# Cross-attention and top-2 expert layer: the loads of expert weights and of later context groups move from SyncE's queue to ScalarE's

## The chip, the cores and the metric

The kernel runs on one core of one Trainium2 chip. The metric is the device time of one execution in microseconds (us). The time before is 1234.87 us, the median of three executions (1233.65 to 1238.93 us). All numbers are 32-bit floats but for a few small masks.

## The reference

64 sequences of 128 tokens, 256 wide. The inputs are `x`, `ctx_1024` and the weights:

```python
x = x + xattn(layernorm(x), ctx, ctx)      # 16 heads of 16; Q, K, V, softmax(QK/4) V, Wo, biases
x = x + ffn(layernorm(x))                  # 8 experts, top 2 of 8 per token
# ffn: silu(x Wg[e]) * (x Wu[e]) -> Wd[e], weighted by a softmax over the two best router probabilities
```

Wg and Wu of one expert are 256 x 512, Wd is 512 x 256: 512 KB each, 24 such matrices in all.

## The kernel before, in words

The program is written for each engine by hand: one instruction list for each, with semaphores between them. Nothing is scheduled by a planner. There are two stages.

**Stage A** takes attention and routing, one sequence `i` after another, in 16 groups `g` of 4 (`b` = `i % 4`). It is unrolled. One turn of TensorE (`stage_a`, L666) is: the scores of `i` (L593), the output projection of `i-2`, the values of the next sequence (or, at `b` = 3, the second half of the next group's queries), the attention product of `i-1` (L618), a transposition of the row maxima (L599), a piece of the next group's keys or queries, transpositions of the next group's normalised `x`, and the scores once more, transposed and less their maxima (L607). A turn takes some 7.6 us.

Scores are computed for heads that lie spread over the partitions. SyncE (SP below) does this spreading by DMA: `spread_keys` and `spread_queries` (L302 to L315, issued at L309) copy `kT` and `qT` of sequence `i+1` into the buffer `heads`, two DMAs each, while TensorE works on `i`. For the first sequence of a group, `qT` is complete only after the second query piece was computed at `b` = 3 and copied by ScalarE (`copy_piece`, L906).

SP's list in stage A (L345 to L364) also has, in this order within a group: at `b` = 1 the store of the finished rows (`out<-x`) and the load of `xT`; at `b` = 2 the load of `x` for group `g+2` (`load_x`, L283), which waits for ScalarE's and GpSimd's last reads of `x_sb`; at `b` = 3, between the keys and the queries, the load of the context of group `g+2` (`load_ctx`, L286), which waits until TensorE has computed the last values of the group (`s_v`); and, at every even `i` from 2 to 48, one of the 24 expert matrices (`load_weight`, L297). All DMAs of one engine go through that engine's own queue: SP's is q1 in the profile, ScalarE's q10, GpSimd's q0. The engines' instructions are fetched on q8 and q14.

ScalarE's list (`stage_a`, L932) has, per sequence: two pieces of a normalisation (L865), the copy of V into `v_aug` (`copy_values`, L912, which waits for the product, `s_v`, and for an attention product), two more pieces of a normalisation, squares (L884), the copy of a key or query piece (L906), of transposed rows (L889), and three exponentials (L918). ScalarE issues only four loads in the kernel before, all at the start (L977, L982).

VectorE takes row maxima (L1084), subtracts them (L1091), turns and divides the attention rows, adds the residual, and at `b` = 3 takes statistics of the `x` that `load_x` brought (`first_stats`, L1056). GpSimd writes the routed rows to memory with indirect DMAs.

TensorE's wait that matters for the pieces is at the head of a turn, ahead of the scores:

```python
                    if i > 0:
                        wait(pe, s_vc, i + 1)
                        wait(pe, s_piece_c, min(4 + i, SEQS))
```

**Stage B**, from about 510 us on, runs the experts over the sorted rows, in units of 256 rows. It needs all 24 matrices (`s_experts`); they are there some 110 us earlier.

Of the kernel before, what the change touches and what calls it, by code (L numbers as in the profile page):

```python
# [15 lines left out]
P = 128  # L16
SEQS, TOK, D = 64, 128, 256
HEADS, DK = 16, 16
EXPERTS, F = 8, 512
GROUP = 4  # L20
GROUPS = SEQS // GROUP
DC = D // P
FC = F // P
# [47 lines left out]
def moe_attention(nc, x, ctxT, wq, bq, wk, bk, wv, bv, wo, bo, router, gating, up, down, xT, woT, out):  # L71
# [4 lines left out]
    with ExitStack() as ctx:  # L76
        def sb(name, shape, dt=fp32):
            return ctx.enter_context(nc.sbuf_tensor(name, shape, dt))

        def sem(name):  # L80
            return ctx.enter_context(nc.semaphore(name))
# [10 lines left out]
        gate_sb = sb("gate_sb", [P, EXPERTS * DC * F])  # L92
        up_sb = sb("up_sb", [P, EXPERTS * DC * F])
        down_sb = sb("down_sb", [P, EXPERTS * FC * D])
# [12 lines left out]
        ctxT_sb = sb("ctxT_sb", [P, 2, DC, GROUP * TOK])  # L107
# [93 lines left out]
        def other_bank(i, k):  # L201
            return banks[:, (0 if i % 2 == 0 else 4) + k]

        s_wk, s_wq, s_wv, s_bias, s_bv, s_bo, s_wo, s_wr, s_experts = (sem(n) for n in (
            "wk_loaded", "wq_loaded", "wv_loaded", "bias_loaded", "bv_loaded", "bo_loaded", "wo_loaded", "router_loaded",
            "experts_loaded"))
        s_bv_rep, s_bvo, s_bias_out = (sem(n) for n in ("bv_repeated", "bv_through_wo", "bias_out_ready"))
        s_x, s_xbo = sem("x_loaded"), sem("x_bo_ready")
        s_ctx = [sem("ctx_loaded_0"), sem("ctx_loaded_1")]
# [10 lines left out]
        s_v, s_vc = sem("values_product"), sem("values_ready")  # L220
# [35 lines left out]
        def wait(eng, semaphore, value):  # L256

            if not isinstance(value, int) or value > 0:
                eng.wait_ge(semaphore, value)
# [21 lines left out]
        def _(sp):  # L281
# [3 lines left out]
            def load_ctx(g, u):  # L285
                sp.dma_start(ctxT_sb[:, u], ctxT[:, bass.ds(g * GROUP * TOK, GROUP * TOK)].rearrange(  # L286
                    "(c p) t -> p c t", p=P)).then_inc(s_ctx[u], 16)

            def load_xT(g):
                wait(sp, s_logitT, g)  # L290
                sp.dma_start(xT_sb[:], xT[:, bass.ds(g * GROUP * TOK, GROUP * TOK)].rearrange("(c p) t -> p c t", p=P)).then_inc(s_xT, 16)

            def load_weight(n):
                e, k = divmod(n, 3)
                w_sb, w, c = ((gate_sb, gating, DC), (up_sb, up, DC), (down_sb, down, FC))[k]
                size = w_sb.shape[1] // EXPERTS
                sp.dma_start(w_sb[:, e * size:(e + 1) * size].rearrange("p (c f) -> p c f", c=c),  # L297
                             w[e:e + 1].rearrange("o (c p) f -> p (o c) f", p=P)).then_inc(s_experts, 16)

            def spread(i, o, src, signal):  # L300

                u, b = i // GROUP % 2, i % GROUP  # L302
# [8 lines left out]
            def spread_keys(i):  # L311
                spread(i, 0, kT, s_kh)

            def spread_queries(i):
                spread(i, 1, qT, s_qh)  # L315
# [29 lines left out]
            def stage_a(g, u, far):  # L345
                for b in range(GROUP):
                    i = g * GROUP + b
                    if 0 < i < SEQS - 1:
                        spread_keys(i + 1)
                    if b == 3 and far:  # L350
                        wait(sp, s_v, g * GROUP + GROUP)
                        load_ctx(g + 2, u)
                    if 0 < i < SEQS - 1:
                        spread_queries(i + 1)
                    if b == 1 and g > 0:
                        store_x1(g - 1)
                    if b == 1 and g + 1 < GROUPS:
                        load_xT(g + 1)
                    if b == 2 and far:
                        wait(sp, s_norm, g + 2)  # L360
                        wait(sp, s_xbo, g + 2)
                        load_x(g + 2)
                    if i % 2 == 0 and 2 <= i < 2 + 2 * 3 * EXPERTS:
                        load_weight(i // 2 - 1)  # L364

            for g in range(GROUPS):
                stage_a(g, g % 2, g + 2 < GROUPS)
# [490 lines left out]
        def _(act):  # L858
# [50 lines left out]
            def copy_values(i, bank):  # L909
                wait(act, s_v, i + 1)  # L910
                wait(act, s_att, i - 2)
                nc.scalar.activation(v_aug[:, i % 3, :, 0:DK], bank[:, 0:D].rearrange("p (h r) -> p h r", r=DK),  # L912
                                     ACT.Copy).then_inc(s_vc, 1)
# [12 lines left out]
            def hold(t, u):  # L926
# [2 lines left out]
                nc.scalar.activation(held[u][:, 0:HALF], gate_sb[:, bass.ds(e * HALF, HALF)], ACT.Copy).then_inc(s_held, 1)  # L929
                nc.scalar.activation(held[u][:, HALF:2 * HALF], up_sb[:, bass.ds(e * HALF, HALF)], ACT.Copy).then_inc(s_held, 1)  # L930

            def stage_a(g, u, core, prev, prev2, prev3, nxt, far):  # L932
                for b in range(GROUP):
                    i = g * GROUP + b
                    one, two = (core if b > 0 else prev), (core if b > 1 else prev)
                    if b == 1 and prev2:
                        router_exp(g - 2)
                    if b == 3 and prev2:
                        gap_exp(g - 2)
                    if b == 0 and nxt and g > 0:  # L940
                        first_norm(g + 1, (0, 1))
                    if nxt and b == 3:
                        copy_piece(g + 1, 1 - u, 3, other_bank(i, 1))
                    if b == 2 and prev:
                        second_norm(g - 1, (0, 1))
                    if b < 3:
                        copy_values(i + 1, other_bank(i, 1))
                    if b == 0 and nxt and g > 0:
                        first_norm(g + 1, (2, 3))
                    if b == 3 and core:  # L950
                        square_x1(i - 3)
                    if i == SEQS - 1:
                        act.wait_ge(s_experts, EXPERTS * 3 * 16)
                        act.wait_ge(s_table, EARLY_STEPS)
                        act.wait_ge(s_kh[1], SEQS // 2 * 32)
                        hold(0, 0)
                    if two and b != 2:
                        square_x1(i - 2)
                    if b == 2 and prev:
                        second_norm(g - 1, (2, 3))  # L960
                    if nxt and b < 3:
                        copy_piece(g + 1, 1 - u, b, other_bank(i, 1))
                    if nxt and b == 3:
                        copy_values(i + 1, other_bank(i, 1))
                    if i == 1:
                        copy_normed(1, 0, other_bank(i, 0))
                        copy_normed(1, 1, other_bank(i, 3))
                    if b < 2 and nxt and g > 0:
                        copy_normed(g + 1, b, other_bank(i, 3))
                    if b == 0 and core:  # L970
                        copy_logitsT(g, other_bank(i, 2))
                    softmax_exp(i)
                    if i == 0:
                        first_norm(1, (0, 1, 2, 3))
# [570 lines left out]
```

## Time and profile before

| | us |
|---|---|
| median of three executions | 1234.87 (1233.65 to 1238.93) |
| the profiled execution, its own time | 1237.15 |
| its span, first to last instruction | 1235.4 |
| TensorE (PE) busy | 1200.5, 97% |
| VectorE busy | 652.1, 53% |
| ScalarE busy | 543.9, 44% |
| GpSimd busy | 425.7, 34% |
| mean granted TensorE clock | 0.994 |

"PE" is the matmul part of TensorE, "PEld" its weight load, which overlaps. "SPq" and "ACTq" are the queues of DMA-issuing instructions of SP and ScalarE; such an instruction's time is the time that the engine's instruction stream is held by it, not the time of the transfer. In a list of instructions, a time in square brackets is idle time ahead of the instruction, with what ended it.

### The profile page before, as it was taken

Reading aid. Unit: us, or ns where it says so; the run is one execution under the profiler, and the core shown is the slowest. Engines: PE = TensorE matmul, PEld = TensorE weight load, DVE = VectorE, ACT = ScalarE, POOL = GpSimd, SP = SyncE. Lnnn points to the kernel's source line nnn. Section 1 sums busy time; section 2 is a strip of 40 time slices with the busy share of each in tenths; the row PEclk is TensorE's granted clock in tenths of the full one; section 3 lists DMA queues with packets and bytes.
Section 4 is the critical chain, followed back from the end, with each engine's and each line's share of the span. In section 5 each row is a group of like instructions: output and inputs, shape, how many; then the busy total and the mean of one; then the engine's idle time right before and its main releaser. Section 6 shows DMA issues by size and latency. Waiting matters only on the chain.

```text
span 1235.4 us, 30330 instructions
## 1 busy us (share of the span) xinstructions
PE 1200.5 (97%) x10994; PEld 980.6 (79%) x10995; DVE 652.1 (53%) x1814; ACT 543.9 (44%) x894; POOL 425.7 (34%) x356
## 2 busy tenths in 40 slices
PE   8999999999999999899999999999999999999996
PEld 6677667676767666688888888888888888888995
DVE  3678888888888888734552222222222222222332
ACT  4566666666666665535422222222222222222442
POOL 3211434433434333253554422222232222222332
PEclk9999999999999999899999999999999999999999
DMA  5554556565555443434444433333333333333432
GB/s 157 153 140 140 174 172 174 173 174 169 175 173 174 136 140 102 96 88 65 78 78 79 68 50 51 51 51 51 51 51 51 51 51 51 51 52 39 57 49 31
DMA packets 176432, 121.07 MB, mean 98 GB/s; under 512 B 103840, under 2 KB 159392, under 8 KB 176320
## 3 DMA queue, kind: packets, MB, share of 16 engines
q1 hardware_dynamic: 148832, 81.41, 27.2%
q0 software_dynamic: 26400, 37.09, 17.2%
q8 instruction: 74, 1.21, 0.4%
q10 hardware_dynamic: 1088, 1.05, 0.3%
q14 instruction: 38, 0.31, 0.1%
HBM read 57.24 MB, written 45.46 MB: 83 GB/s over the span
## 4 chain that ended last, share of the span: by engine, by line
PE 91%; DVE 3%; DMA 2%; issue 1%; SPq 1%; ACT 0%; POOL 0%; POOLq 0%; DVEq 0%
PE banks L564 74%; PE banks L593 5%; PE banks L607 5%; PE banks L618 4%; DMA heads<-qT 2%; PE banks L599 1%; DVE row_max L1084 1%; PE banks L570 1%; SPq L309 1%; DMA out<-x_sb,token 1%; PE banks L647 1%; PE banks L747 0%; ACT qT L906 0%; DMA ends<-sorted_x 0%; DVE q_less L1091 0%
## 5 line engine op out<-in xcount | busy, mean ns | idle before, releaser
L513 POOL DMA_INDIRECT out<-x_sb,token x135 | 210.6, 1560 | 418.3 <-DVE x_sb L1434 376.5
L924 ACT ACTIVATE qT<-banks 128x1024 f32<-128x1024 f32 (+1 forms) x75 | 70.4, 939 | 468.9 <-PE banks L564 447.6
L1428 DVE TENSOR_TENSOR heads<-qT,banks 128x1024 f32<-128x1024 f32 (+1 forms) x75 | 83.6, 1115 | 343.5 <-PE banks L564 335.6
L564 PE MATMUL banks<-down_sb,heads 128*128 x1080 | 245.5, 379 | 0.9 <-DVE heads L1428 0.9
L564 PE MATMUL banks<-xnT,kT 128*128 128x256 f32 (+1 forms) x1216 | 244.1, 359 | 0.0
L564 PE MATMUL banks<-xnT,probs 128*128 128x256 f32 (+1 forms) x1184 | 238.4, 359 | 0.0
L564 PEld LDWEIGHTS banks<-xnT,kT 128*128 128x128 f32 x1216 | 213.1, 191 | 25.9 <-issue 0.2
L564 PEld LDWEIGHTS banks<-xnT,probs 128*128 128x128 f32 x1184 | 208.4, 190 | 25.1
L564 PEld LDWEIGHTS banks<-down_sb,heads 128*128 128x128 f32 x1080 | 204.0, 190 | 28.2 <-issue 1.1
L462 POOL DMA_INDIRECT sorted_x<-xn,slots_now x128 | 125.6, 981 | 258.5 <-PE banks L618 82.9
L1084 DVE TENSOR_REDUCE row_max<-banks 128x16 f32<-128x2048 f32 x64 | 146.6, 2290 | 32.5 <-PE banks L593 32.0
L918 ACT ACTIVATE probs<-banks 128x512 f32<-128x512 f32 (+1 forms) x192 | 128.1, 740 | 46.8 <-PE banks L607 46.8
L1434 DVE TENSOR_SCALAR x_sb<-banks,weight 128x256 f32<-128x256 f32 x135 | 59.8, 480 | 123.6 <-PE banks L564 106.3
L593 PE MATMUL banks<-heads 32*128 32x128 f32 x2048 | 74.6, 282 | 9.3 <-DMA heads<-qT 5.4
L607 PEld LDWEIGHTS banks<-q_less,heads 32*128 32x128 f32 x2048 | 64.1, 189 | 19.4 <-issue 16.9
L607 PE MATMUL banks<-q_less,heads 32*128 32x128 f32 x2048 | 76.5, 286 | 1.0 <-DVE q_less L1091 1.0
L593 PEld LDWEIGHTS banks<-heads 32*128 32x128 f32 x2048 | 65.4, 188 | 14.8 <-issue 14.2
L564 PE MATMUL banks<-wo_sb,attnT 128*128 128x265 f32 x256 | 74.6, 414 | 0.0
L618 PEld LDWEIGHTS banks<-probs,v_aug 128*32 128x32 f32 x2048 | 52.0, 109 | 27.7 <-issue 27.0
L618 PE MATMUL banks<-probs,v_aug 128*32 128x128 f32 x2048 | 69.2, 276 | 0.0
L564 PE MATMUL banks<-wv_sb,ctxT_sb 128*128 128x256 f32 x256 | 65.9, 380 | 0.4 <-ACT probs L918 0.4
L1091 DVE TENSOR_TENSOR q_less<-heads,banks 128x256 f32<-128x256 f32 x128 | 48.1, 418 | 33.6 <-PE banks L599 17.2
(187 smaller groups left out, 1237.5 us busy)
## 6 DMA issues: line engine op xcount, KB each, us to landing
xn<-sorted_x SPq DMA_DIRECT2D x240, 64.0 KB
x_sb<-in_x SPq DMA_DIRECT2D x16, 512.0 KB, 4.0
ctxT_sb<-in_ctx SPq DMA_DIRECT2D x16, 512.0 KB
heads<-kT SPq DMA_DIRECT2D x128, 64.0 KB
heads<-qT SPq DMA_DIRECT2D x128, 64.0 KB
xT_sb<-in_xT SPq DMA_DIRECT2D x16, 512.0 KB, 5.5
out<-x SPq DMA_DIRECT2D x16, 512.0 KB
gate_sb<-_L_ffn_kernel_gating_EDF SPq DMA_DIRECT2D x8, 512.0 KB
```

The source lines that it names most:

```text
L462: pool.indirect_dma_start(out=sorted_x[:, :], out_offset=bass.IndirectOffsetOnAxis(ap=slots_now[:, g % 2, i:i + 1], axis=0), in_=xn2[:, g ...
L513: pool.indirect_dma_start(out=out[:, :], out_offset=bass.IndirectOffsetOnAxis(ap=token[:, v, h:h + 1], axis=0), in_=ys[:, 2 * u + h, :], i ...
L564: last = nc.tensor.matmul(dst, lhsT, rhs, start=(i == 0), stop=(i == len(pairs) - 1))
L593: last = nc.tensor.matmul(score_banks(i)[:, j, c * TOK:(c + 1) * TOK], q_heads[strip(j), i % 2, c, :], k_heads[strip(j), i % 2, c, :], sta ...
L607: last = nc.tensor.matmul(score_banks(i)[:, j, c * TOK:(c + 1) * TOK], k_heads[strip(j), i % 2, c, :], q_less[strip(j), c, :], start=True, ...
L618: last = nc.tensor.matmul(bank[32 * j:32 * j + 32, q * TOK:(q + 1) * TOK], v_aug[:, i % 3, 4 * q + j, :], probs[:, j, c, :], start=True, s ...
L918: nc.scalar.activation(probs[:, j:j + n].rearrange("p j h t -> p j (h t)"), score_banks(i)[:, j:j + n], ACT.Exp, scale=DK ** -0.5).then_in ...
L924: nc.scalar.activation(gatedT[:, 0:w * F], all_banks[:, 1024 * place:1024 * place + w * F], ACT.Silu).then_inc(s_silu, 1)
L1084: nc.vector.reduce_max(row_max[:].rearrange("p (j r a) -> p j r a", r=16, a=2)[:, :, 0:4, 1], score_banks(i).rearrange("p j (h t) -> p j h ...
L1091: nc.vector.tensor_tensor(q_less[:, c:c + 2, :], q_heads[:, i % 2, c:c + 2, :], bank[:, 0:TOK].unsqueeze(1).broadcast_to([P, 2, TOK]), ALU ...
L1428: nc.vector.tensor_tensor(fusedT[:, u, 0:w * F], gatedT[:, 0:w * F], gate_up[:, 1024:1024 + w * F], ALU.mult).then_inc(s_fuse, 1)
L1434: last = nc.vector.tensor_scalar(ys[:, 2 * u + h, :], work[:, 0, h * D:(h + 1) * D], weight[:, v, h:h + 1], None, ALU.mult)
```

## The change

`load_weight` and `load_ctx` are issued by ScalarE in stage A, right behind `copy_values`. SP no longer issues the 24 expert matrices nor the contexts of groups 2 to 15; it keeps those of groups 0 and 1. The wait on `s_v` ahead of SP's `load_ctx` goes; `copy_values` has just waited for the same semaphore and value. The context load moves from `b` = 3 to `b` = 2.

```diff
-            def load_weight(n):
...
-                sp.dma_start(w_sb[:, e * size:(e + 1) * size].rearrange("p (c f) -> p c f", c=c),
-                             w[e:e + 1].rearrange("o (c p) f -> p (o c) f", p=P)).then_inc(s_experts, 16)
...
-                    if b == 3 and far:
-                        wait(sp, s_v, g * GROUP + GROUP)
-                        load_ctx(g + 2, u)
...
-                    if i % 2 == 0 and 2 <= i < 2 + 2 * 3 * EXPERTS:
-                        load_weight(i // 2 - 1)
...
+            def load_weight(n):
...
+                act.dma_start(w_sb[:, e * size:(e + 1) * size].rearrange("p (c f) -> p c f", c=c),
+                              w[e:e + 1].rearrange("o (c p) f -> p (o c) f", p=P)).then_inc(s_experts, 16)
+
+            def load_ctx(g, u):
+                act.dma_start(ctxT_sb[:, u], ctxT[:, bass.ds(g * GROUP * TOK, GROUP * TOK)].rearrange(
+                    "(c p) t -> p c t", p=P)).then_inc(s_ctx[u], 16)
...
                     if b < 3:
                         copy_values(i + 1, other_bank(i, 1))
+                    if b == 2 and far:
+                        load_ctx(g + 2, u)
+                    if i % 2 == 0 and 2 <= i < 2 + 2 * 3 * EXPERTS:
+                        load_weight(i // 2 - 1)
```

In SP's list before, at `b` = 2 and `b` = 3 of group 1, to the queries of the next group's first sequence (`heads` is the spread buffer):

```order
L309 DMA heads<-kT 64x256 x2
L309 DMA heads<-qT 64x256 x2
L283 DMA x_sb<-in_x 128x4x256
L297 DMA down_sb<-in_L_ffn_kernel_down_EFD 128x4x256
L309 DMA heads<-kT 64x256 x2
L286 DMA ctxT_sb<-in_ctx 128x2x512
L309 DMA heads<-qT 64x256 x2
```

The same place in SP's list of the changed kernel (its L302 is L309 of before):

```order
L302 DMA heads<-kT 64x256 x2
L302 DMA heads<-qT 64x256 x2
L283 DMA x_sb<-in_x 128x4x256
L302 DMA heads<-kT 64x256 x2
L302 DMA heads<-qT 64x256 x2
```

Between the `x` load and the group's last queries, a weight load and a context load have left SP's list.

ScalarE's list of the changed kernel at `b` = 2 of group 1, from the normalisation to the query copy (its L853, L900, L894 are L865, L912, L906 of before):

```order
L853 ACTIVATE xn<-x,shift,rstd 128x2x4x32 x2
L900 ACTIVATE v_aug<-banks 128x16x16
L928 DMA ctxT_sb<-in_ctx 128x2x512
L924 DMA down_sb<-in_L_ffn_kernel_down_EFD 128x4x256
L853 ACTIVATE xn<-x,shift,rstd 128x2x4x32 x2
L894 ACTIVATE qT<-banks,bq_sb 128x4x128
```

The two DMA rows are new there; the two normalisation pieces and the query copy are behind them. The rest of the list and TensorE's list keep their order.

## Rows read from the trace of the kernel before

**Rows 1.** The page, busy time of the engines.
```profile
PE 1200.5 (97%) x10994; PEld 980.6 (79%) x10995; DVE 652.1 (53%) x1814; ACT 543.9 (44%) x894; POOL 425.7 (34%) x356
```
**Rows 2.** Waits of PE, 0 to 560 us: total, times, longest.
```profile
PE banks L593 <- DMA heads<-qT: 5.4, 7, 1.6
```
**Rows 3.** Busy time by stretch: groups 4 and 5, from scores to scores.
```profile
143.80:175.03 31.23, 30.33 (x466) 21.48 (x467) 27.02 (x80) 20.42 (x43) 12.91 (x12) 1.00 0.59 171
175.03:205.57 30.54, 30.32 (x467) 21.48 (x467) 25.73 (x77) 19.07 (x41) 11.71 (x11) 1.00 0.59 174
```
**Rows 4.** PE in order of time: scores that open a group.
```profile
52.36 1.17 PE L593 MATMUL banks<-heads 32*128 32x128 f32 x32 [0.83 <-DMA heads<-qT]
...
143.82 1.17 PE L593 MATMUL banks<-heads 32*128 32x128 f32 x32 [0.18 <-issue]
175.03 1.17 PE L593 MATMUL banks<-heads 32*128 32x128 f32 x32 [0.85 <-DMA heads<-qT]
...
298.68 1.17 PE L593 MATMUL banks<-heads 32*128 32x128 f32 x32 [1.57 <-DMA heads<-qT]
...
360.15 1.17 PE L593 MATMUL banks<-heads 32*128 32x128 f32 x32 [0.42 <-DMA heads<-qT]
...
422.36 1.17 PE L593 MATMUL banks<-heads 32*128 32x128 f32 x32 [1.21 <-DMA heads<-qT]
```
**Rows 5.** The chain of waits ahead of two such scores.
```profile
80.48 2.02 DMA heads<-qT
...
294.85 3.69 DMA heads<-qT
```
**Rows 6.** SP's queue, group 1 at b=3, then group 4 at b=2 and b=3.
```profile
76.62 1.42 SPq L286 DMA_DIRECT2D ctxT_sb<-in_ctx  x1
79.96 1.11 SPq L309 DMA_DIRECT2D heads<-qT  x2
...
164.05 0.37 SPq L283 DMA_DIRECT2D x_sb<-in_x  x1
...
168.12 0.59 SPq L286 DMA_DIRECT2D ctxT_sb<-in_ctx  x1
171.43 1.10 SPq L309 DMA_DIRECT2D heads<-qT  x2
```
**Rows 7.** DMA queues, 172.2 to 172.6 us: packets, MB, share of 16 engines.
```profile
q8 instruction: 1, 0.02, 16.9%
```
**Rows 8.** DMA queues, 76.4 to 76.8 us.
```profile
q8 instruction: 1, 0.02, 17.5%
```
**Rows 9.** DMA queues, 162.5 to 163.1 us.
```profile
q8 instruction: 1, 0.02, 15.2%
```
**Rows 10.** DMA queues, 285.6 to 286.0 us.
```profile
q8 instruction: 1, 0.02, 21.0%
```
**Rows 11.** ScalarE in order of time, group 4, b=2.
```profile
162.75 0.39 ACT L912 ACTIVATE v_aug<-banks 128x256 f32<-128x256 f32 x1
163.03 1.09 ACT L865 ACTIVATE xn<-x,shift,rstd 128x256 f32<-128x256 f32 x2
165.79 0.69 ACT L906 ACTIVATE qT<-banks,bq_sb 128x512 f32<-128x512 f32 x1 [1.67 <-PE banks L564]
```
**Rows 12.** PE in order of time, the scores behind that copy.
```profile
166.69 1.17 PE L593 MATMUL banks<-heads 32*128 32x128 f32 x32
```
**Rows 13.** ScalarE in order of time, group 5, b=0.
```profile
181.19 0.69 ACT L906 ACTIVATE kT<-banks,bk_sb 128x512 f32<-128x512 f32 x1 [1.14 <-issue]
```
**Rows 14.** DMA issues by line: duration ns min/median/max, first and last start.
```profile
L977 ACTq DMA_DIRECT2D wq_sb<-in_L_xattn_Wq x1: 563/563/563, 1.3 to 1.3; - x1
...
L286 SPq DMA_DIRECT2D ctxT_sb<-in_ctx x14: 578/587/1420, 45.7 to 446.6; - x14
```
**Rows 15.** The line of the x loads, issue to landing.
```profile
DMA to landing us min/median/max: 3.8/4.0/5.1
```
**Rows 16.** VectorE in order of time, group 4, b=3.
```profile
170.13 0.74 DVE L1056 BATCH_NORM_STATS2 stats<-x_sb 128x6 f32<-128x256 f32 x2
```
**Rows 17.** Busy time by stretch, one microsecond; the last column is GB/s.
```profile
168.00:169.00 1.00, 1.00 (x5) 0.85 (x5) 1.00 (x1) 1.00 (x3) 0.31 (x1) 1.00 1.12 376
```

More of the change, by code:

```diff
@@ L291, in load_xT @@
                 sp.dma_start(xT_sb[:], xT[:, bass.ds(g * GROUP * TOK, GROUP * TOK)].rearrange("(c p) t -> p c t", p=P)).then_inc(s_xT, 16)
-            def load_weight(n):
-                e, k = divmod(n, 3)
-                w_sb, w, c = ((gate_sb, gating, DC), (up_sb, up, DC), (down_sb, down, FC))[k]
-                size = w_sb.shape[1] // EXPERTS
-                sp.dma_start(w_sb[:, e * size:(e + 1) * size].rearrange("p (c f) -> p c f", c=c),
-                             w[e:e + 1].rearrange("o (c p) f -> p (o c) f", p=P)).then_inc(s_experts, 16)
             def spread(i, o, src, signal):
@@ L930, in hold @@
                 nc.scalar.activation(held[u][:, HALF:2 * HALF], up_sb[:, bass.ds(e * HALF, HALF)], ACT.Copy).then_inc(s_held, 1)
+            def load_weight(n):
+                e, k = divmod(n, 3)
+                w_sb, w, c = ((gate_sb, gating, DC), (up_sb, up, DC), (down_sb, down, FC))[k]
+                size = w_sb.shape[1] // EXPERTS
+                act.dma_start(w_sb[:, e * size:(e + 1) * size].rearrange("p (c f) -> p c f", c=c),
[3 more added lines that the diff above has]
+                    "(c p) t -> p c t", p=P)).then_inc(s_ctx[u], 16)
             def stage_a(g, u, core, prev, prev2, prev3, nxt, far):
```

## The prediction

> **What bounds the kernel now.** I read the page first: TensorE is busy for 1200.5 us of 1235.4, and ScalarE for only 44% [rows 1]. So a change of queues can give back at most what TensorE spends waiting, and costs something only where it makes TensorE wait. The change touches stage A alone; the expert matrices are complete long before stage B needs them, and stage B's lists are the same. So I asked next for what TensorE waits for in stage A. Beside start and end, one wait is on a transfer: the scores on the spread queries, 5.4 us in 7 waits [rows 2]. The list of TensorE in order of time shows where: only at the first scores of a group, with 0.83, 0.85, 1.57, 0.42 and 1.21 us idle ahead of them; the other such scores have 0.18 us (one row stands for eight, 0.18 to 0.21), which the profile lays on no transfer [rows 4]. Two neighbouring groups show that such a wait reaches the end: 31.23 us with the wait of 0.85, 30.54 without, with 30.33 and 30.32 us of TensorE work and the clock granted in full in both [rows 3].
>
> The reason for the place is in the order of the work. The last queries of a group are ready late, SP spreads them at once (171.43), and nothing else is left for TensorE to do until they land. In SP's queue the load of the next context stands ahead of them by 3.3 us (168.12) [rows 6]. That is what the change takes away, and the question is whether the context load is what makes the queries late.
>
> **Part 1, the queries without a context load ahead.** The rows say mostly no. The shortest flight of the queries is 2.02 us, behind the first issue at 79.96, and there the context load was closest of all: its issue ended at 78.04, 1.9 us before [rows 5, 6]. The longest, 3.69 us, comes at a boundary with the usual 3.3 us between them [rows 5]. What goes with the long flights is a packet of 16 KB on q8, an instruction fetch. The window 172.2 to 172.6 has one; 16.9% of 16 engines times 0.4 us is 1.08 us of one DMA engine [rows 7]. I looked at the windows of the four long waits (0.83, 0.85, 1.57, 1.21) and found one in each, and none where the queries flew for 2.0 us. A fetch holds one of 16 engines, and the queries need their share from all 16. The fetches follow TensorE's instruction stream, which stays as it is, so these four waits stay. Only the wait of 0.42 us has no fetch beside the queries but one at 355 us, beside the context load, whose packets on that engine then stand ahead of the queries. It should fall to the 0.18 of the others: **-0.2 us**. The bounds: nothing, or all five down to 0.18, which is 4.88 less 0.90, **-4.0 us**. I take -0.2, since the shortest flight had the context load closest.
>
> By the Trainium skill, page "DMA: Bandwidth & Descriptors", section "Issuing engines are not separate DMA queues", DMAs from any engine run on the same 16 DMA engines, and issuing them from several saves only the issue time, which would make this part 0. No run here shows that yet.
>
> **Part 2, SP's list gets shorter.** 24 weight loads and 14 context loads go, 38 issues of about 0.59 us [rows 14], 22 us in all. SP is not on TensorE's path with them: it waits for ScalarE before the queries at 171.43, and the context issue had ended at 168.71 [rows 6]. **0 us**; if SP had no such slack, at most the same 4.0 us of waits could go.
>
> **Part 3, ScalarE holds for 38 issues.** An issue on ScalarE's queue took 0.56 us at the start, the context issue on SP 0.59 in the median [rows 14]. At `b` = 0 one is put in, 0.6 us, ahead of idle time of 1.14 us before the key copy [rows 13]: hidden, **0 us**. At `b` = 2 of most groups two are put in, 0.59 + 0.56 and two gaps of 0.04, **1.2 us**. Behind them stand two normalisation pieces, and then the query copy at 165.79 with 1.67 us of idle time ahead [rows 11]: hidden too, but with 0.45 us left. This cover is thin and leads straight to TensorE: the copy ends at 166.48, and the scores that need it start at 166.69 [rows 12], so 0.2 us more and TensorE waits.
>
> It is used up where an issue takes long. SP's context issue at 76.62 took 1.42 us, 0.83 more than the median [rows 6, 14], and a fetch of 1.12 us began beside it (17.5% of 16 engines times 0.4 us) [rows 8]. So an issue that meets a fetch is held until about its end. At ScalarE's new place, this happens in group 4: a fetch of 1.46 us begins between 162.5 and 163.1, and the copy of V ends at 163.14 [rows 9, 11]. Sixteen sequences later, in group 8, a fetch of 1.34 us begins between 285.6 and 286.0 [rows 10]. In each the pair takes 1.2 and another 0.8 (as at 76.62) to 1.2 us (scaled by the fetch's length), 2.0 to 2.4 in all; less 1.67 of idle and up to 0.2 behind the copy, TensorE waits 0.1 to 0.7 us. I take 0.4, twice: **+0.8 us**. The bounds of the whole part: 0, if issue and copy of V overlap fully; the upper end is rival B's.
>
> **Part 4, the loads meet others.** The context load is now issued about 163.1, 0.9 us before the load of `x` at 164.05, and the weight load beside it. The `x` load lands 4.0 us after its issue, 168.05, and VectorE needs it at 170.13 [rows 6, 15, 16]. A microsecond of full traffic moves 376 GB/s, so 512 KB take 1.4 us [rows 17]. If the packets of `x` alternate with those of the context, `x` lands 1.4 us later at most, 0.7 us in time: **0 us**.
>
> **The sum**: -0.2 + 0 + 0.8 + 0 = **+0.6 us**. On the profiled execution's own time of 1237.15 us (span 1235.4 and 1.75 around it) that is 1237.8. That execution lies 2.3 us above the median of the runs shown, 1234.87, so I forecast **1235.5 us**. What a measurement of this kernel can tell from no change is about 0.5%, 6.2 us: this counts as no difference.
>
> **The rivals.** **A: the private queue frees the queries.** If the fetch hurts because context packets still wait on the held engine, or if the packets of context and queries stood in one row, all five waits fall to 0.18: -4.0, part 3 adds 0 to 0.8, so 1231 to 1232 us. Were the nine gaps of 0.18 to go also, another 1.6, 1229.3. For it: the wait of 0.42. Against it: the flight of 2.02 us right behind a context load. The Trainium skill, page "DMA: Bandwidth & Descriptors", section "Queues, rings and completion order", has each engine take turns between the rows of its rings packet by packet, and on one row in order, which would be this rival; the shortest flight speaks against it. Chance 0.2.
>
> **B, on the other side: ScalarE's issues are long.** The place is `b` = 2, the price what a pair takes beyond 1.67 + 0.2 us. If a ScalarE issue between activations costs what the slowest of SP's context loads took, 1.42, a pair takes 2.9 and each of 12 groups loses 1.0 us: 1234.87 + 12 = 1247 us. It decides from a pair of 2.4 us on, where 12 times 0.5 makes 0.5%. For it: no row shows ScalarE issuing between activations. Against it: its issues at the start, 0.56. Chance 0.07.
>
> **C, slower also: `x` is late.** If `x` is served only after context and weights, it comes 2.8 us later, 6.8 after its issue instead of the 6.1 that VectorE leaves, and 14 groups lose 0.7 us: 1245 us. VectorE's statistics stand ahead of the subtraction that TensorE waits for, so it would show at once. It decides from 6.5 us on. Against it: the two queues would have to be served unequally. Chance 0.05.
>
> **D: nothing moves.** ScalarE absorbs also the fetches; 1234.7. I count it with the forecast.
>
> **How the numbers follow.** Forecast with D 0.63, A 0.2, B 0.07, C 0.05, and 0.05 for what I have not seen, split evenly. The forecast's own range, with 1 us either way for the median of few runs, is 1234 to 1237. The range that should hold 8 in 10 takes in A down to its -4.0 and leaves B and C out: 1230.5 to 1240.0. Faster by over 0.5% is 0.03, since even A with all gaps gone stays inside; slower by over 0.5% 0.12; the rest, 0.85, is the same.
>
> **What would show it.** In the changed kernel's waits of TensorE, the wait on the spread queries should keep about 5 us; with rival A it is near 0. In ScalarE's list at `b` = 2, two issues of 0.6 us stand behind the copy of V, and the idle time ahead of the query copy falls from 1.67 to about 0.45; in groups 4 and 8 it is gone, an issue takes over 1.2 us, and the scores of the fourth sequence start late by some tenths. B would show as long issues in every group, C as a wait of VectorE on `x` (L1056). The forecast is wrong if the long flights vanish while fetches are still beside them, or if TensorE waits at `b` = 3 in most groups.

## The result, and the profile after

The changed kernel takes **1242.09 us** (median of six executions, 1239.3 to 1248.53); the kernel before, in the same session, 1234.9 (six, 1233.23 to 1238.93). The ratio is 1.0053, 95% interval 1.0036 to 1.007: slower by half a per cent. The forecast of 1235.5 was wrong, and its range ended at 1240.0. The profiled execution of the changed kernel is its longest, 1248.53 us.

The page of the changed kernel, busy time of the engines, against [rows 1]:

```profile
PE 1206.4 (97%) x10994; PEld 984.5 (79%) x10995; DVE 652.1 (52%) x1814; ACT 546.0 (44%) x894; POOL 425.2 (34%) x356
```

TensorE is busy 5.9 us longer with the same 10994 matmuls. The view of cores has the reason, a lower mean clock (0.994 before):

```profile
core 0: 1246.8 us, clock 0.987
```

The span has grown by 11.4 us, 5.9 of it slower TensorE work and the rest waits. The waits of TensorE, 0 to 560 us, against [rows 2]:

```profile
PE banks L647 <- DVE q_less L1094: 7.1, 4, 2.4
...
PE banks L581 <- DMA heads<-qT: 2.9, 4, 1.4
...
PE banks L595 <- DVE q_less L1094: 1.7, 3, 0.6
```

The wait on the spread queries (L581, L593 of before) has halved, and a new one of 7.1 us stands above it: the matmul that counts the places of the routed rows (L647) waits for VectorE's subtraction (L1094). VectorE's own waits, 20 to 560 us, say what holds it, and its list in order of time where:

```profile
DVE stats L1059 <- DMA x_sb<-in_x: 8.9, 5, 2.6
```

```profile
80.98 0.75 DVE L1059 BATCH_NORM_STATS2 stats<-x_sb 128x6 f32<-128x256 f32 x2 [1.09 <-DMA x_sb<-in_x]
...
174.67 0.75 DVE L1059 BATCH_NORM_STATS2 stats<-x_sb 128x6 f32<-128x256 f32 x2 [1.78 <-DMA x_sb<-in_x]
...
206.18 0.75 DVE L1059 BATCH_NORM_STATS2 stats<-x_sb 128x6 f32<-128x256 f32 x2 [1.11 <-DMA x_sb<-in_x]
...
300.11 0.75 DVE L1059 BATCH_NORM_STATS2 stats<-x_sb 128x6 f32<-128x256 f32 x2 [2.33 <-DMA x_sb<-in_x]
...
334.23 0.75 DVE L1059 BATCH_NORM_STATS2 stats<-x_sb 128x6 f32<-128x256 f32 x2 [2.55 <-DMA x_sb<-in_x]
```

Before, the statistics never waited for `x` from 20 us on. Now they do in 5 of the 14 groups that load one. The chain of waits through the last of these places shows the whole mechanism, from the read of `x_sb` that the load waits for to TensorE:

```profile
323.09 2.37 POOL x_bo L443
...
325.52 8.68 DMA x_sb<-in_x
...
334.23 0.04 DVE stats L1059
...
335.99 0.06 DVE q_less L1094
...
336.70 0.19 PE banks L647
...
336.99 1.72 PE banks L595 x32
```

The `x` load flies for 8.68 us; its median was 4.0 and its longest flight 5.1 [rows 15]. What it meets is in the lists of the two issuing engines, ScalarE first, then SP:

```profile
324.21 0.38 ACT L900 ACTIVATE v_aug<-banks 128x256 f32<-128x256 f32 x1
324.21 0.37 ACTq L928 DMA_DIRECT2D ctxT_sb<-in_ctx  x1
324.62 0.53 ACTq L924 DMA_DIRECT2D gate_sb<-_L_ffn_kernel_gating_EDF  x1
```

```profile
325.52 0.37 SPq L283 DMA_DIRECT2D x_sb<-in_x  x1
328.43 1.10 SPq L302 DMA_DIRECT2D heads<-kT  x2
```

Context and weight are issued 1.3 and 0.9 us ahead of `x`. The DMA queues say how the three are served. From 325.5 to 328.0 us:

```profile
q10 hardware_dynamic: 360, 0.70, 89.9%
```

From 329.0 to 331.5 us:

```profile
q1 hardware_dynamic: 617, 0.59, 70.0%
q0 software_dynamic: 45, 0.13, 12.5%
q10 hardware_dynamic: 10, 0.01, 1.4%
```

For the first 2.5 us after its issue the `x` load has no finished packet on q1, SP's queue; ScalarE's q10 fills the engines. Then the shares are reversed. With nothing ahead of it, in the kernel before at 164.05, q1 finished 234 packets in the first 2.5 us. So at this place the loads do not alternate: `x` is served when the earlier ones are nearly done, though they stand on another queue.

That order alone does not make `x` late, though. At 230.53 the first 2.5 us after the issue look the same, and VectorE did not wait:

```profile
q10 hardware_dynamic: 348, 0.68, 91.0%
q1 hardware_dynamic: 3, 0.00, 0.1%
```

At 325.52, too, nearly all of `x` is in by 331.5, 6.0 us after the issue, when VectorE leaves 6.1. From 328.0 to 331.5 us q1 moved 0.63 MB of the 0.66 that `x` and the keys behind it have, and from 331.5 to 333.0 us next to nothing, beside an instruction fetch (4.2% of 16 engines times 1.5 us, 1.0 us of one of them):

```profile
q1 hardware_dynamic: 663, 0.63, 56.2%
```

```profile
q8 instruction: 1, 0.02, 4.2%
q1 hardware_dynamic: 7, 0.01, 1.8%
```

The load raises its semaphore in parts, up to 16, and VectorE waits for the last. The trace has the times of 13 parts of this load: twelve came within 5.96 us of the issue, the last after 8.68. In the groups at 73.19, 166.74 and 198.91 it is much the same: all but one or two of the recorded parts within 5.2 to 6.5 us, the last after 7.8, 7.9 and 7.3. At 291.60 it is another picture: seven of 15 parts come after more than 6.7 us, and in the first 2.5 us q1 finishes 141 packets beside 259 of q10, so there the two loads do run side by side. In the nine groups without a long wait the last part is in after at most 6.2 us. So the two loads ahead use up nearly all the time in hand, and the loss is made by the parts of `x` that come later than the rest.

What such a place costs is read from the two turns of TensorE around it. Changed kernel, sequences 39 and 40, from scores to scores; the column behind the counts is the granted clock:

```profile
328.15:338.48 10.33, 7.91 (x123) 5.73 (x118) 7.02 (x23) 4.13 (x10) 2.58 (x3) 0.94 0.43 143
338.48:347.46 8.98, 8.98 (x136) 6.66 (x132) 6.59 (x20) 6.28 (x13) 2.38 (x3) 0.88 0.47 120
```

The same two turns before:

```profile
321.60:329.28 7.68, 7.50 (x122) 5.18 (x115) 6.78 (x23) 4.37 (x11) 2.38 (x3) 1.00 0.83 263
329.28:337.33 8.05, 8.05 (x129) 5.84 (x133) 6.80 (x20) 6.05 (x13) 2.58 (x3) 1.00 0.43 136
```

The first turn is 2.65 us longer, 2.24 of it more idle time (2.42 against 0.18) and 0.41 slower work. The second is 0.93 longer with no idle time at all: the clock is at its lower level, 1.2 instead of 2.4 GHz, for part of it. The granted clock falls behind the idle 2.4 us:

```profile
333.00:337.00 4.00, 1.57 (x22) 1.01 (x14) 2.77 (x9) 1.22 (x5) 0.96 (x1) 1.00 0.25 73
337.00:341.00 4.00, 4.00 (x66) 3.74 (x67) 2.48 (x13) 2.23 (x4) 1.04 (x1) 0.57 0.15 37
```

I compared the start of all 64 scores in the two lists. The delay grows by 0.60 us in group 1, 1.01 in 4, 1.00 in 5, 1.04 and 0.93 around sequence 36, 2.65 and 0.93 around 40: **8.2 us** at the five places where the statistics wait for `x`. Another 1.5 us comes at 33 to 37 us and 1.6 behind the scores at 432.38, both stretches at the low clock; 1.0 in groups 2 and 3 has no such cause, and small gains take 0.5 off. In a second session the changed kernel's profile repeats the first kind and not the other two (below), and the medians differ by 7.2 us.

### The profile page after: what moved, and what is told of

Read it like the earlier page. It is cut to its first block, busy times and chain, and to the rows that moved or that the text cites. A ratio compares the mean times of both kernels' runs of the same rounds, so it can differ in the third digit from the quotient of the medians.

```text
span 1246.8 us, 30330 instructions
## 1 busy us (share of the span) xinstructions
PE 1206.4 (97%) x10994; PEld 984.5 (79%) x10995; DVE 652.1 (52%) x1814; ACT 546.0 (44%) x894; POOL 425.2 (34%) x356
## 4 chain that ended last, share of the span: by engine, by line
PE 86%; DMA 5%; DVE 5%; issue 1%; SPq 1%; POOL 1%; ACT 0%; POOLq 0%; DVEq 0%
PE banks L552 70%; PE banks L595 4%; PE banks L581 4%; PE banks L606 4%; DMA x_sb<-in_x 3%; PE banks L587 1%; DVE row_max L1087 1%; DMA heads<-qT 1%; PE banks L558 1%; POOL x_bo L443 1%; SPq L302 1%; PE banks L635 1%; DMA out<-x_sb,token 1%; DVE stats L1059 1%; DVE q_less L1094 1%
## 5 line engine op out<-in xcount | busy, mean ns | idle before, releaser
L912 ACT ACTIVATE qT<-banks 128x1024 f32<-128x1024 f32 (+1 forms) x75 | 70.4, 938 | 469.1 <-PE banks L552 447.8
L906 ACT ACTIVATE probs<-banks 128x512 f32<-128x512 f32 (+1 forms) x192 | 128.1, 740 | 52.7 <-PE banks L595 52.7
L581 PE MATMUL banks<-heads 32*128 32x128 f32 x2048 | 76.7, 287 | 6.8 <-DMA heads<-qT 2.9
L581 PEld LDWEIGHTS banks<-heads 32*128 32x128 f32 x2048 | 67.5, 194 | 11.9 <-issue 11.7
L1094 DVE TENSOR_TENSOR q_less<-heads,banks 128x256 f32<-128x256 f32 x128 | 48.1, 417 | 34.7 <-PE banks L587 18.7
(187 smaller groups left out, 1239.3 us busy)
```

The source lines that it names most:

```text
L581: last = nc.tensor.matmul(score_banks(i)[:, j, c * TOK:(c + 1) * TOK], q_heads[strip(j), i % 2, c, :], k_heads[strip(j), i % 2, c, :], sta ...
L906: nc.scalar.activation(probs[:, j:j + n].rearrange("p j h t -> p j (h t)"), score_banks(i)[:, j:j + n], ACT.Exp, scale=DK ** -0.5).then_in ...
L912: nc.scalar.activation(gatedT[:, 0:w * F], all_banks[:, 1024 * place:1024 * place + w * F], ACT.Silu).then_inc(s_silu, 1)
L1094: nc.vector.tensor_tensor(q_less[:, c:c + 2, :], q_heads[:, i % 2, c:c + 2, :], bank[:, 0:TOK].unsqueeze(1).broadcast_to([P, 2, TOK]), ALU ...
```

## The experiments

Three theories at first. **Place** (P): it counts only what is issued ahead of what; with context and weight ahead of `x`, `x` lands late. **Queue** (Q): ScalarE's own queue is favoured over SP's. **S:** ScalarE is held by issuing, whatever the order. Each ratio compares with the kernel before as it ran beside that version; its medians are 1232.88 to 1235.96 us.

### One load at a time

Context loads on ScalarE at `b` = 2, the weights back on SP behind `x`. Against the changed kernel:

```diff
...
                         load_x(g + 2)
+                    if i % 2 == 0 and 2 <= i < 2 + 2 * 3 * EXPERTS:
+                        load_weight(i // 2 - 1)
...
                         load_ctx(g + 2, u)
-                    if i % 2 == 0 and 2 <= i < 2 + 2 * 3 * EXPERTS:
-                        load_weight(i // 2 - 1)
```

> Theory P (place): x lands late because a context load and a weight load are issued ahead of it at b=2, whatever the queue. Here the context alone is ahead of it, the weight behind it: x lands about 1.4 us later than before, near 5.4 us after its issue, before the 6.1 us that VectorE leaves; no wait on x, the time within 2 us of before (ratio 0.998 to 1.002). The four waits on the spread queries beside an instruction fetch stay, 4 to 5 us in all, though no context load is ahead of them. Theory Q (queue): ScalarE's queue is served ahead of SyncE's; then the same here, since only one load is ahead. Theory S (ScalarE is held by its issues, and that is what costs): 14 of 38 issues remain on ScalarE, a third of the loss, +2 to +3 us.

Measured: 1235.32 against 1235.96 us, ratio 0.9994 (0.9984 to 1.0003). One load of 512 KB ahead of `x` does no harm that the time shows: VectorE waits for `x` in 4 places, 1.8 us in all and 0.8 at most, where I had expected no wait. Nor does it help the queries that no context load stands ahead of them now; against [rows 2], the same span of time:

```profile
PE banks L590 <- DMA heads<-qT: 4.7, 7, 1.2
```

Weights alone on ScalarE, the context again on SP at `b` = 3:

```diff
+                    if b == 3 and far:
+                        wait(sp, s_v, g * GROUP + GROUP)
+                        load_ctx(g + 2, u)
...
-                    if b == 2 and far:
-                        load_ctx(g + 2, u)
```

> The context load stays with SyncE at b=3, the weights go to ScalarE. Theory P: one load ahead of x, x in time, ratio 0.998 to 1.003; the wait on the spread queries as before. Theory S: 24 of 38 issues on ScalarE, two thirds of the loss, +4 to +5 us, and ScalarE's copies late.

Measured: 1235.98, ratio 1.0001 (0.999 to 1.0012), with the wait on the queries as before, 5.2 us, and one wait on `x`, 1.0 us. Neither half of the change costs anything that can be told from none. They cost only together.

### Both loads ahead of `x`, on SP's queue

Nothing on ScalarE. Against the kernel before:

```diff
-                    if b == 3 and far:
-                        wait(sp, s_v, g * GROUP + GROUP)
-                        load_ctx(g + 2, u)
...
                     if b == 2 and far:
+                        wait(sp, s_v, g * GROUP + GROUP)
+                        load_ctx(g + 2, u)
+                    if b == 2 and i < 2 + 2 * 3 * EXPERTS:
+                        load_weight(i // 2 - 1)
+                    if b == 2 and far:
                         wait(sp, s_norm, g + 2)
                         wait(sp, s_xbo, g + 2)
                         load_x(g + 2)
-                    if i % 2 == 0 and 2 <= i < 2 + 2 * 3 * EXPERTS:
+                    if b == 0 and 2 <= i < 2 + 2 * 3 * EXPERTS:
                         load_weight(i // 2 - 1)
```

> Nothing is issued by ScalarE; SyncE issues context and weight at b=2 ahead of x. Theory P: x is as late as in the change or later (7 to 9 us after its own issue in the groups with a fetch), ratio 1.003 to 1.008. Theory Q: if ScalarE's queue were favoured, x would here stand in the same queue in plain order and the loss would be another one; a ratio near 1.000 would speak for Q. Theory S: no ScalarE issue, ratio 1.000.

Measured: 1240.54 against 1235.96, ratio 1.0034 (1.0023 to 1.0046). VectorE and TensorE wait for the same things, with no ScalarE issue in the kernel:

```profile
DVE stats L1058 <- DMA x_sb<-in_x: 10.9, 10, 2.4
```

```profile
PE banks L661 <- DVE q_less L1093: 4.8, 5, 2.3
```

Most of the slowdown is there without the second queue and without an issue on ScalarE, so neither **queue** nor **S** is its main cause. The ratio is below the changed kernel's 1.0053, but the intervals overlap; whether the rest is the queue's stays open. This profile has one stretch at the low clock between 20 and 490 us (180 to 183); the changed kernel's has four.

### All 38 on ScalarE, but the weights one sequence later

```diff
-                    if i % 2 == 0 and 2 <= i < 2 + 2 * 3 * EXPERTS:
-                        load_weight(i // 2 - 1)
+                    if b == 1 and 3 <= i < 3 + 2 * 3 * EXPERTS:
+                        load_weight((i - 1) // 2 - 1)
...
+                    if b == 3 and 3 <= i < 3 + 2 * 3 * EXPERTS:
+                        load_weight((i - 1) // 2 - 1)
```

> All 38 issues stay on ScalarE, the weights one sequence later (b=1 and b=3), so that the context alone is ahead of x. Theory P: no wait on x, ratio 0.997 to 1.002. Theory Q: the same. Theory S: the loss stays, ratio 1.004 to 1.007.

Measured: 1238.02 against 1235.96, ratio 1.0013 (0.9999 to 1.0026). VectorE waits once for `x`, 1.1 us, and TensorE 4.8 us for the queries. With every issue still on ScalarE, most of the cost is gone; what is left can't be told from none.

### A third load ahead of `x`

```diff
-                    if i % 2 == 0 and 2 <= i < 2 + 2 * 3 * EXPERTS:
-                        load_weight(i // 2 - 1)
+                    if b == 2 and i < 2 + 2 * 3 * EXPERTS:
+                        for n in range(g * 2, min(g * 2 + 2, 3 * EXPERTS)):
+                            load_weight(n)
```

> The change, with both weight loads of a group ahead of x at b=2 (context, weight, weight), none at b=0. Theory P, one more load of 1.4 us ahead of x: x lands 7 to 8 us after its issue in all 12 groups with weights, VectorE waits 1 to 2 us in each, TensorE also: +12 to +24 us against before, ratio 1.010 to 1.020. If x shared the engines evenly with the loads ahead, it would land hardly later than in the change and the ratio stays near 1.005.

Measured: 1255.73 against 1232.88, ratio 1.0183 (1.0162 to 1.0205). The line of the `x` loads, and the waits of VectorE and of TensorE, 20 to 560 us:

```profile
DMA to landing us min/median/max: 4.8/7.4/9.8
```

```profile
DVE stats L1060 <- DMA x_sb<-in_x: 16.0, 10, 3.1
```

```profile
PE banks L647 <- DVE q_less L1095: 13.5, 9, 3.0
```

One load ahead costs nothing, two 0.5%, three 1.8%: `x` has to wait for each in turn until the time that VectorE leaves is used up. Had `x` shared the engines evenly, the third load would have changed little, as the expectation says.

### Taking `x` off the path: the statistics behind the subtraction

```diff
-                    if b == 3 and far:
-                        first_stats(g + 2, (0, 1))
...
-                    if b == 3 and far:
-                        first_stats(g + 2, (2, 3))
...
                     take_max_off(i, other_bank(i, 3))
+                    if b == 3 and far:
+                        first_stats(g + 2, range(GROUP))
```

> The change, with VectorE's statistics of x placed behind its subtraction of the maxima at b=3 instead of ahead of it. Theory P says that the late x costs only because the subtraction, for which TensorE waits, stands behind the statistics. Here x is as late (up to 8.7 us after its issue) but nothing that TensorE needs soon is behind it: TensorE's waits of 1.0 to 2.4 us ahead of the places product (b=3) go, and the loss with them, ratio 0.998 to 1.002. The attention rows of b=3 come 1.5 us later, which may cost up to 1 us in a group. If the loss came from elsewhere (bandwidth taken from other transfers, ScalarE), it stays: 1.004 to 1.007.

Measured: 1250.76, ratio 1.0129 (1.0114 to 1.0145), a miss. The waits on `x` are gone, and a larger one is new:

```profile
PE banks L581 <- DVE place L1184: 16.4, 11, 1.5
```

The statistics now delay the next thing on VectorE that TensorE waits for, the reading of the places, in 11 groups. This run can't prove the path from `x` to TensorE; the chain above and the runs around it have to carry that.

### Both loads behind `x`

The two issues at `b` = 2 go behind the query copy. Against the changed kernel:

```diff
-                    if b == 2 and far:
-                        load_ctx(g + 2, u)
-                    if i % 2 == 0 and 2 <= i < 2 + 2 * 3 * EXPERTS:
+                    if b == 0 and 2 <= i < 2 + 2 * 3 * EXPERTS:
                         load_weight(i // 2 - 1)
...
                         copy_piece(g + 1, 1 - u, b, other_bank(i, 1))
+                    if b == 2 and far:
+                        load_ctx(g + 2, u)
+                    if b == 2 and i < 2 + 2 * 3 * EXPERTS:
+                        load_weight(i // 2 - 1)
```

> The change, with the two issues at b=2 moved behind ScalarE's copy of the query piece, some 2.7 us later and 1.7 us behind the issue of x. Theory P, service in the order of issue over both queues: x lands 4.0 us after its issue as before, no wait of VectorE on it, ratio 0.998 to 1.002. If the queues shared the engines evenly, x would still be slowed by up to 1 us. If the gain from clearing b=3 is real, the queries' flights at b=3 are as in the kernel with the context alone moved, 4 to 5 us of waits in all.

Measured: 1237.05 against 1232.88, ratio 1.0029 (1.0017 to 1.0041). The line of the `x` loads, and the wait on the queries, 20 to 560 us:

```profile
DMA to landing us min/median/max: 3.8/3.9/5.2
```

```profile
PE banks L581 <- DMA heads<-qT: 10.1, 11, 1.6
```

`x` is in time again, as expected. The time is above what I expected, and that the wait on the queries would stay at 4 to 5 us was a miss. I read it so that the crowd of transfers was moved, not removed, and now ends on the keys and queries of the next group; no run tests this apart.

A run between the two keeps before's order as nearly as ScalarE's list allows: context at `b` = 3, the weight of `b` = 2 behind the query copy.

```diff
+                    if b == 3 and far:
+                        load_ctx(g + 2, u)
...
-                    if b == 2 and far:
-                        load_ctx(g + 2, u)
-                    if i % 2 == 0 and 2 <= i < 2 + 2 * 3 * EXPERTS:
+                    if b == 0 and 2 <= i < 2 + 2 * 3 * EXPERTS:
                         load_weight(i // 2 - 1)
...
+                    if b == 2 and i < 2 + 2 * 3 * EXPERTS:
+                        load_weight(i // 2 - 1)
```

> ScalarE issues all 38 loads, but at about the times at which SyncE issued them before: the context at b=3 ahead of the last query copy, the weight of b=2 behind the query copy, so both behind x. Theory P (place, not queue): x lands after 4.0 us, no wait on it, the waits on the spread queries as before, 4 to 6 us; ratio 0.998 to 1.002. If ScalarE's queue as such costs something, the ratio is above 1.002.

Measured: 1238.5 against 1235.88, ratio 1.0023 (1.0009 to 1.0036), above what I expected, with 9.1 us of waiting for the queries, 20 to 560 us, in 11 places. The weight is issued about 1.3 us later than before. Whether this delay alone makes the queries late, or a private queue adds to it, this run does not separate; the two runs with one load at a time speak against a cost of the queue as such.

### Do the fetches make the queries late?

Part 1 of the prediction rests on this. 64 empty instructions at the head of TensorE's list were to move its later fetches:

```diff
+            for _ in range(64):
+                pe.nop(nofuse=True)
             pe.wait_ge(s_masks, 1)
```

> The kernel before, with 64 instructions that do nothing ahead of TensorE's list, which shifts every later instruction fetch of TensorE. If the waits on the spread queries at 52, 175, 299 and 422 us come from a fetch beside them, they go from these groups and turn up in others where a fetch now falls, or in none; ratio 0.997 to 1.003. If they come from the place in the program (context load ahead, routing), they stay at the same four groups.

It told nothing: the built program had no more TensorE instructions than before. As a repeat of the kernel before it gave 1.0002 (0.9991 to 1.0013), which shows how well the comparison repeats. The second try has 16 more warm-up matmuls, most of them narrow:

```diff
-            for _ in range(12):
-                nc.tensor.matmul(banks[:, 6, 0:P], ident[:], ident[:], start=True, stop=True)
+            for k in range(28):
+                n = P if k < 8 else 8
+                nc.tensor.matmul(banks[:, 6, 0:n], ident[:], ident[:, 0:n], start=True, stop=True)
```

> The kernel before, with 8 wide and 20 narrow warm-up products in place of 12 wide ones, so that TensorE's list behind them stands some 64 instructions later against its fetches (the instructions that do nothing of the run before this one had left the program, so it told nothing). If the waits on the spread queries at 52, 175, 299 and 422 us come from a fetch beside them, they leave these groups, for others or none; if they come from the place in the program they stay. Ratio 0.996 to 1.003.

Measured: 1245.26 against 1235.88, ratio 1.0078 (1.0055 to 1.01), higher than expected. The first scores start 6.2 us later (25.60 against 19.40); the other 3 us I have not traced. The places are what the run is for. TensorE's scores that open a group, in order of time:

```profile
88.85 1.17 PE L593 MATMUL banks<-heads 32*128 32x128 f32 x32 [0.97 <-DMA heads<-qT]
...
338.72 1.17 PE L593 MATMUL banks<-heads 32*128 32x128 f32 x32 [1.43 <-DMA heads<-qT]
...
369.69 1.17 PE L593 MATMUL banks<-heads 32*128 32x128 f32 x32 [0.59 <-DMA heads<-qT]
```

In [rows 4] the long waits stand at 52, 175, 299 and 422 us. Here they stand at 88.85, 213.30, 338.72 and 462.56: one group on (30 to 31 us), beside the 6 to 9 us by which this kernel runs late. The short wait at 360.15 stays in its group (369.69). The edit moves TensorE's instructions in its list and leaves every load and spread at its place in its group, so the fetches choose the groups in which the queries are late by 0.8 us and more.

### The changed kernel once more, and a try at a better one

> The change once more, for a second profile. Theory P: VectorE waits on x in 4 to 7 groups, 6 to 12 us in all; ratio 1.003 to 1.008. The number of stretches at half clock in stage A, of which the first profile has five and the kernel before one, should be lower where the waits of TensorE are shorter.

Measured: 1243.59 against 1235.88, ratio 1.0049 (1.0032 to 1.0066). The profile has the same new waits of TensorE and VectorE (6.5 us in 4 places and 8.2 in 7, 20 to 560 us), and the low clock again around 302 and 336 us. The stretches at 35 and 434 us are not there, so they are no steady part of the change.

The last run joins the harmless half of the change (context on ScalarE) with fewer warm-up matmuls, to move the fetches off the queries. Against the first experiment:

```diff
-            for _ in range(12):
+            for _ in range(4):
                 nc.tensor.matmul(banks[:, 6, 0:P], ident[:], ident[:], start=True, stop=True)
```

> The kernel with only the context load moved, and 4 warm-up products in place of 12, which puts TensorE's list some 32 instructions earlier against its fetches, half the shift of the run before. If a fetch hurts the queries only in a narrow part of b=3, this shift may meet it in fewer groups than four: each that is spared gives 0.4 to 1.2 us. Ratio 0.995 to 1.002; if the four waits of 0.8 us and more only move on, 0.999 to 1.001. Fewer warm-up products may leave the first products at the lower clock, up to 2 us more.

Measured: 1234.66 against 1234.26, ratio 1.0004 (0.9995 to 1.0014). The wait on the queries is down to 3.2 us, but the first scores start 2.1 us later than before. No version here beats the kernel before.

## Why the prediction was wrong

**Part 4 failed**, at the sentence "If the packets of `x` alternate with those of the context, `x` lands 1.4 us later at most, 0.7 us in time". Three things were wrong in it. I priced one load of 512 KB, though two are ahead. I had them alternate, and at 325.52 the queues show service nearly in order of issue. But even that order gives a landing in time: the context lands 4.0 us after its issue, the two loads behind it take 1.4 us each, and from the issue at 324.21 this makes 331.0, 5.5 us after `x`'s issue and inside the 6.1. The step that broke is "at most". I took a load for one thing that lands at one time, while VectorE waits for its last part, and in five groups that came 7.3 to 8.7 us after the issue, 3.3 to 4.7 later than the 4.0 of before. The term was set at 0; the waits on `x` measure 8.9 us and TensorE's delays at these places 8.2 us in the profiled execution.

**Rival C** is what happened in its cause (service after context and weights), its place, its sign and its path to TensorE. That its 1245 us is only 3 above the median is luck. It charges both loads in full, 2.8 us, though they have a start of 1.3 us on `x`; with that start its own rule gives 5.5 us and no loss. Measured are not 14 groups at 0.7 us, but five at 1.1 to 2.6 us of VectorE waiting for `x`, and the clock on top. In the other nine `x` was in time. Against it I had put that "the two queues would have to be served unequally", and gave it 0.05. Order of issue over both queues is such a service. The late and the timely flights do lie on the two sides of its decision point of 6.5 us: 7.3 and more, 6.2 and less.

**Part 1 was right in its mechanism.** Without a context load ahead the wait on the queries stays at 4.7 us, and moving the fetches moves the waits. In the changed kernel it falls to 2.9 us, but in groups 4 and 8 TensorE already arrives late by the wait on `x` at `b` = 3: the same delay, paid elsewhere. The -0.2 for the wait of 0.42 us has no support: that wait is gone with the context moved, but also with the weights alone moved and the context still ahead. Rival A (0.2) falls: of the kernels that move half of the loads or all of them, none gains.

**Part 2 was right:** SP's shorter list frees nothing, by the same runs.

**Part 3 found the collision and missed the overlap.** ScalarE's list in group 4, at the place of [rows 11]:

```profile
165.47 0.38 ACT L900 ACTIVATE v_aug<-banks 128x256 f32<-128x256 f32 x1 [0.15 <-PE banks L552]
165.48 0.38 ACTq L928 DMA_DIRECT2D ctxT_sb<-in_ctx  x1
165.89 1.44 ACTq L924 DMA_DIRECT2D down_sb<-in_L_ffn_kernel_down_EFD  x1
167.43 1.10 ACT L853 ACTIVATE xn<-x,shift,rstd 128x256 f32<-128x256 f32 x2 [1.57 <-issue]
168.48 0.69 ACT L894 ACTIVATE qT<-banks,bq_sb 128x512 f32<-128x512 f32 x1
```

The weight issue met the fetch and took 1.44 us, as forecast. But the context issue runs beside the copy of V and holds ScalarE for 0.38 instead of 0.59, so the pair takes 1.85 instead of 2.0 to 2.4 us. The scores behind the query copy start at 169.37 with their delay against before unchanged, and so do those in group 8: +0.8 was 0. That was the part's lower bound. Rival B falls too: most weight issues take 0.5 to 0.8 us. Its chance and C's with half of the unseen make 0.145, where the prediction has 0.12 for slower by over 0.5%.

By the Trainium skill, page "DMA: Bandwidth & Descriptors", section "Issuing engines are not separate DMA queues", DMAs of all issuing engines run on the same 16 DMA engines. The runs agree: the changed kernel and the one with all issues on SP are both slower, by 0.5% and 0.3%. The same page's section "Queues, rings and completion order" has a DMA engine take turns between its rows packet by packet. At 325.52 the trace shows no such turns between q10 and q1 for 2.5 us (89.9% of the engines' time on q10, no finished packet on q1); at 291.60 packets of both finish side by side. Where page and measurement differ, the measurement decides; whether `x`'s packets already stood in their row at 325.52, no run shows.

**How much of the slowdown is explained.** The five places carry 8.2 us of the profiled pair, the medians differ by 7.2. That the low clock follows the longest waits, around 302 and 336 us, is seen in two executions of the changed kernel; no run took the clock away with the wait left in place. Why the last parts of `x` are late in these five groups and not in the other nine stays open. In groups 4 and 8 the weight issue met a fetch and took 1.44 and 1.37 us. In the other three a fetch runs while `x` flies, but so it does in groups where `x` is in time, and no run moved the fetches with both loads ahead.

## What to carry to other kernels

A load that is moved earlier is moved ahead of others on the same DMA engines, on whatever queue it stands. List every transfer issued in the few microseconds around it, sum their bytes in order of issue at the measured rate, and compare each landing with the time its reader leaves. Then ask for a margin for the last part of the load: here one load of 1.4 us fitted into the 2.1 us in hand, and two, with their start of 1.3 us, fitted by some 0.6 us on paper and in nine of 14 groups, but the last parts were up to 3.2 us later than that sum. A transfer that nobody waits for soon, like these weights, belongs behind the ones with a deadline; but there, too, something comes next, and the run with both loads behind `x` has more waiting for the queries.

## What I had not expected of the hardware

- Transfers of two engines' queues were at most places served nearly in order of issue: at 325.52 no packet finished on q1 for 2.5 us while q10's two loads ran, at 89.9% of the engines' time. At 291.60, where the weight issue had met a fetch, they ran side by side.
- A load of 512 KB can be in but for one part and wait for that: at 325.52 twelve of 13 recorded parts came within 5.96 us, the last after 8.68.
- A DMA issue on ScalarE ran beside the activation ahead of it (165.48 beside 165.47, both 0.38 us). In the first experiment all 14 context issues there took 374 or 375 ns. SP's had a median of 587 [rows 14], but 435 in the run that issues both loads early on SP, so part of the difference is the place and not the engine.
- Behind a wait of 2.4 us on TensorE its clock fell from 2.4 to 1.2 GHz (granted clock 1.00 from 333 to 337 us, 0.57 from 337 to 341), and the two turns lost 1.3 us more than the wait. Behind a wait of 1.65 us at 177.14 it did not fall (1.00 from 177 to 181).
